# Attention on one NeuronCore: the exponential of a step taken head by head, each PSUM bank of the turned scores released by itself, layer-norm statistics one step later

## The chip, the cores and the metric

The kernel runs on one NeuronCore of a Trainium2 chip. The metric is the device time of one execution in microseconds (us). The engines are TensorE (PE; PEld is its weight load), VectorE (DVE), ScalarE (ACT), GpSimd (POOL) and SyncE (SP, which here only issues DMAs). They run side by side and wait for each other by semaphores.

## The reference

Two blocks, each of a cross attention and a feed-forward part, with layer norm ahead of each and a gain by tanh. The change lies in the first attention:

```python
# x, ctx_2048: (64, 64, 256) fp32; x is (batch, channel, position)
x = x + tanh(g_xattn[0]) * _L0_xattn_ref(_layernorm(x, axis=-1), ctx_2048, Wq, bq, Wk, bk, Wv, bv, Wo, bo)

def _L0_xattn_ref(x, c, ...):                 # 8 heads of 8 channels
    q, k, v = _proj(Wq, bq, x), _proj(Wk, bk, c), _proj(Wv, bv, c)
    q, k = _rope(q, 4), _rope(k, 4)           # per head, over 256 positions
    scores = einsum('bhqd,bhkd->bhqk', q, k) / sqrt(8)
    out = einsum('bhqk,bhkd->bhqd', softmax(scores), v)
    return _proj(Wo, bo, out)
```

Behind it follow a mixture of 8 experts (2 taken) with a shared one, a gated recurrent unit with pooled context, and a feed-forward part with a Hadamard rotation. The change leaves these alone.

## The kernel before, in words

**Tiles and steps.** Two batches make a tile of 128 rows (`TILES` = 32). A tile has 16 heads (8 of each batch), two to a step, so `STEPS` = 8 steps, called p = 0 to 7. Each engine walks through all tiles and steps with its own program (`body(n, c, i)`). Work on a tile is spread over several passes: in pass n, k and v come from tile n + 3 and n + 2, q from n + 2, plain scores from n + 1, turned scores from n or n − 1 (`LAG` = 5 steps behind), values two steps behind those, output of n − 2. Thirteen passes are written out (`PEEL_FIRST`, `PEEL_LAST`); 24 tiles run in a hardware loop of four passes a turn, where thresholds of semaphores are computed in registers.

**Scores twice.** A head's scores are computed in two layouts. *Plain*, with queries on partitions, into `s_ps` (two buffers of two PSUM banks): VectorE takes their row maximum (`take_max`, L400). *Turned*, with keys on partitions, into `st_ps` (one buffer, two banks, one a head): ScalarE takes the exponential into `e_t` (L461 to L468), with the maximum already taken off by rows of the stacked operand. TensorE then multiplies `e_t` by the values into `o_ps` (`use_values`, L557). The contraction of a score has 32 rows, so a head sits in one of four 32-row groups of TensorE's array; a step's two heads are in neighbouring groups, and the turned and plain heads of a step in different ones.

**TensorE's order in a step** (`score_step`, L531, then `use_values`, then one odd job on the bank `misc`). It waits until the exponential of the step before is done (all of `st_ps` is read) and until a buffer of `s_ps` is free, then issues eight matmuls: two turned (first half of the rows, both heads), two plain, two turned (second half), two plain. `st_scored` and `scored` go up once a step, with the last matmul of each kind. The odd jobs: p = 0 and 4 turn o (L577), p = 1 turns the maxima (L599), p = 2 projects q and p = 5 projects k (L508), p = 3 turns a (L617), p = 6 projects the output (L638), p = 7 projects v (L647).

**VectorE in a step**: the row maximum of two heads (L406, 128x1024), and around it at p = 0 the splitting of the maxima (L395, L397) and o's scaling (L412, L416), at p = 2 the layer-norm statistics of tile n + 3 (`stats_of`, L354) and behind them the rotary product of q (L387), at p = 4 o's scaling, at p = 5 the rotary product of k.

**ScalarE in a step**: the exponential, and behind it at p = 1 the copy of the maxima (L473), at p = 2 and 6 the copy of o (L478), at p = 3 that of a (L482), at p = 6 the output (L486), at p = 7 the copy of v (L494). Every second exponential also waits for `pv_done`, so that its buffer of `e_t` is free.

**POOL** normalizes and splits q's and k's inputs (L275, L301); **SP** issues the DMAs that stack q and k in row groups, and waits for `st_scored` of a whole tile ahead of overwriting a stacked buffer (L228, L256).

Of the kernel before, what the change touches and what calls it, by code (L numbers as in the profile page):

```python
# [19 lines left out]
HEADS, DH = 8, 8  # L20
# [47 lines left out]
def attention(nc, dram, x, ident, tanh_gain):  # L68
# [17 lines left out]
    with ExitStack() as ctx:  # L86
# [107 lines left out]
        def _(sp):  # L194
# [20 lines left out]
            def body(n, c, i):  # L215
# [9 lines left out]
                if there(n, c, 2):  # L225
                    r = (c + 2) % RING

                    wait_count(sp, s["st_scored"], STEPS * (n - 1))  # L228
                    if isinstance(n, int) and n == -2:
                        sp.wait_ge(s["q_first_cleared"], 1)  # L230
                    elif isinstance(n, int) and n < 2:
                        sp.wait_ge(s["q_cleared"], n + 2)
                    wait_alone(sp)
                    sp.dma_start(q_st[r][MAX_ROWS, :, :].bitcast(F32), zero_rows[:, :, :].bitcast(F32))\
                        .then_inc(q_stacked[r], 16)
# [17 lines left out]
                if there(n, c, 3):  # L253
                    r = (c + 3) % RING

                    wait_count(sp, s["st_scored"], STEPS * n)  # L256
                    sp.wait_ge(s["k_high"], n + 4)
# [87 lines left out]
        def _(dve):  # L345
# [76 lines left out]
            def body(n, c, i):  # L422
                for p in range(STEPS):
# [4 lines left out]
                    if p == 0 and there(n, c, -2):  # L428
                        normalize_out(n - 2, 1)
                    if p == 2 and there(n, c, 3):  # L430
                        stats_of(n, c, i, 3)
# [23 lines left out]
        def _(act):  # L455
# [3 lines left out]
            def body(n, c, i):  # L459
                for p in range(STEPS):  # L460
                    k, t = later(p, LAG)  # L461
                    if there(n, c, k):
                        g = STEPS * (n + k) + t
                        act.wait_ge(s["st_scored"], g + 1)
                        if t % 2 == 0:
                            wait_count(act, s["pv_done"], 2 * UNITS * (n + k) + 2 * (t // 2) - 2)
                        nc.scalar.activation(e_t[t % 4][:], st_ps[:], ACT.Exp, scale=float(DH) ** -0.5)\  # L467
                            .then_inc(s["exp_done"], 1)  # L468
                    if p == 1 and there(n, c, 0):
# [31 lines left out]
        def _(pe):  # L501
# [10 lines left out]
            def scores(c, p):  # L512

                r = (c + 1) % RING
                for half_ in range(2):
                    for at in range(2):
                        u, j = (2 * p + at) // UH, (2 * p + at) % UH
                        rows = slice(32 * j, 32 * j + 32)
                        yield (s_ps[p % 2][:, at, half_, :], q_st[r][rows, u, half_ * P:(half_ + 1) * P],
                               k_st[r][rows, u, :])  # L520

            def scores_turned(c, k, t):

                r = (c + k) % RING
                for half_ in range(2):
                    for at in range(2):
                        u, j = (2 * t + at) // UH, (2 * t + at) % UH
# [3 lines left out]
            def score_step(n, c, i, p):  # L531
# [3 lines left out]
                if turned:  # L535
                    if t == 0:
                        pe.wait_ge(m_stacked[(c + k) % RING], 16 * uses(c, i, k))
                    wait_count(pe, s["exp_done"], STEPS * (n + k) + t)
                    wait_alone(pe)
                if plain:  # L540
# [8 lines left out]
                    wait_count(pe, s["max_taken"], (n + 1) * STEPS + p - 1)  # L549
                for at in range(0, 4, 2):  # L550
                    for of, done in ((turned, "st_scored"), (plain, "scored")):
                        for out, w, moving in of[at:at + 2]:
                            last = nc.tensor.matmul(out, w, moving, start=True, stop=True)  # L553
                        if of and at == 2:
                            last.then_inc(s[done], 1)

            def use_values(n, c, p):  # L557

                k, t = later(p, LAG + 2)
                if there(n, c, k):  # L560
                    r, u, half_ = (c + k) % RING, t // 2, t % 2
                    if half_ == 0:
                        pe.wait_ge(s["exp_done"], STEPS * (n + k) + 2 * u + 2)
                        if u == 0:
# [1741 lines left out]
```

## Time and profile before

| | |
|---|---|
| median of 3 runs | 1506.12 us (1505.72 to 1512.41) |
| the profiled execution, in all | 1498.02 us |
| its span, from first to last instruction | 1496.0 us |
| PE, DVE, ACT, POOL busy over the span | 89%, 62%, 50%, 46% |
| exponentials (L467) | 256 of 1026 ns |
| row maxima (L406) | 256 of 1222 ns |
| mean granted TensorE clock | 0.964 |

Busy shares are means over four stages with different limits, and matmuls are pipelined, so that PE's share is no measure of its room. Attention is the stage up to about 513 us; what a change there is worth is read from its steps. The profile puts a step's records in order of time: start, length, engine, line, operation, what it writes and reads, and in brackets idle time ahead of it with what ended it.

### The profile page before, as it was taken

The page shows a single profiled execution, that of the slowest core. Times are in us where ns is not written, and L with a number is a line of the kernel's source. Part 1 is how long each engine was busy: PE and PEld are TensorE (multiplying, and loading weights), DVE is VectorE, ACT ScalarE, POOL GpSimd, SP SyncE. Part 2 cuts the span into 40 slices and gives each one's busy share as a digit, 9 for nine tenths or more (in the row PEclk, how much of TensorE's full clock was granted, in tenths as well). Part 3 has the DMA queues.
Part 4 walks back from the last instruction along what each step waited for, and adds up shares of the span by engine and source line. Part 5 has one row for each costly group of instructions (what it writes and reads, how often), then busy time and mean ns, then how long its engine had stood idle before and what let it go on. Part 6 is the DMA issues. An engine that isn't in the chain of part 4 may idle for free. (4 is left out here: it accounts for less than half of the span.)

```text
span 1496.0 us, 31398 instructions
## 1 busy us (share of the span) xinstructions
PE 1335.2 (89%) x10082; PEld 1003.1 (67%) x10083; DVE 925.2 (62%) x1685; ACT 753.8 (50%) x1205; POOL 683.2 (46%) x850
## 2 busy tenths in 40 slices
PE   4898999999998759999898999999957799999998
PEld 3444444444454348887787888888855688888887
DVE  7788888888898268665654333333324566666653
ACT  0477776777777643332343333333324666666652
POOL 7576767676764027544465433200044444554220
PEclk9999999999999969999999999999965899999999
DMA  3222222222221022111654333211161011111000
GB/s 99 81 72 79 71 79 71 78 77 76 79 74 48 3 90 99 47 53 68 193 178 159 95 95 91 69 51 53 46 216 29 7 36 43 43 28 43 15 15 29
DMA packets 88480, 107.61 MB, mean 72 GB/s; under 512 B 11280, under 2 KB 79248, under 8 KB 87760
## 3 DMA queue, kind: packets, MB, share of 16 engines
q1 hardware_dynamic: 78656, 74.57, 15.8%
q0 software_dynamic: 9744, 31.99, 6.7%
q8 instruction: 47, 0.77, 0.2%
q14 instruction: 33, 0.27, 0.1%
HBM read 54.10 MB, written 25.03 MB: 53 GB/s over the span
## 5 line engine op out<-in xcount | busy, mean ns | idle before, releaser
L406 DVE TENSOR_REDUCE row_max<-s_ps 128x4 f32<-128x1024 f32 x256 | 312.2, 1222 | 49.5 <-PE s_ps L553 44.5
L467 ACT ACTIVATE e_t<-st_ps 128x1024 f32<-128x1024 f32 x256 | 262.7, 1026 | 140.3 <-PE st_ps L553 140.3
L553 PE MATMUL st_ps<-q_st,k_st 32*128 32x256 f32 x1024 | 130.8, 331 | 45.6 <-DVE row_max L406 18.6
L569 PE MATMUL o_ps<-e_t,v_st 128*32 128x256 f32 x2048 | 166.2, 397 | 0.0
L553 PEld LDWEIGHTS st_ps<-q_st,k_st 32*128 32x128 f32 x1024 | 80.3, 187 | 103.9 <-issue 65.0
L1731 POOL DMA_INDIRECT gathered_tail<-sorted_results,result_at x64 | 70.3, 1098 | 154.1 <-POOLq L2222 135.8
L553 PE MATMUL s_ps<-k_st,q_st 32*128 32x256 f32 x1024 | 130.7, 342 | 5.9 <-DVE row_max L406 3.6
L1968 DVE TENSOR_TENSOR h_all_tail<-silu_tail,u_ps_tail 128x512 f32<-128x512 f32 x64 | 43.9, 685 | 122.0 <-ACT silu_tail L1839 66.7
L1589 PE MATMUL y_ps_moe<-w_all_moe,xt_hi_moe 128*128 x568 | 112.2, 281 | 4.7 <-DVE xt_lo_moe L1407 4.7
L1413 DVE TENSOR_TENSOR h_all_moe<-silu_moe,u_ps_moe 128x512 f32<-128x512 f32 x71 | 48.8, 687 | 108.9 <-PE u_ps_moe L1567 108.9
L1091 ACT COPY y_sb_moe<-y_ps_moe 128x256 f32<-128x256 f32 x71 | 26.5, 373 | 163.0 <-PE y_ps_moe L1589 163.0
L1567 PE MATMUL g_ps_moe<-w_all_moe,xt_hi_moe 128*128 x284 | 106.8, 417 | 0.0
L1567 PE MATMUL u_ps_moe<-w_all_moe,xt_hi_moe 128*128 x284 | 101.2, 397 | 0.0
L1589 PEld LDWEIGHTS y_ps_moe<-w_all_moe,xt_hi_moe 128*128 128x128 f32 x568 | 91.8, 188 | 8.4 <-issue 5.6
L929 POOL DMA_INDIRECT sorted_rows<-xn_moe,slots_moe x64 | 64.0, 1000 | 57.3 <-DVE slots_moe L1202 40.0
L1403 DVE TENSOR_TENSOR xt_lo_moe<-t_ps_moe,xt_hi_moe 128x256 fp32r<-128x256 f32 x71 | 30.1, 424 | 92.3 <-ACT xt_hi_moe L1078 92.3
L553 PEld LDWEIGHTS s_ps<-k_st,q_st 32*128 32x128 f32 x1024 | 77.7, 193 | 7.8 <-DVE row_max L406 4.9
L1839 ACT ACTIVATE silu_tail<-g_ps_tail 128x512 f32<-128x512 f32 x64 | 38.0, 594 | 84.0 <-PE g_ps_tail L2127 83.8
L1589 PE MATMUL y_ps_moe<-w_all_moe,xt_lo_moe 128*128 x284 | 79.5, 280 | 0.0
L304 POOL TENSOR_TENSOR q_bare<-q_roped 128x256 f32<-128x256 f32 x32 | 23.2, 726 | 112.2 <-DVE q_roped L387 112.2
L2139 PE MATMUL y_ps_tail<-w_hi_tail,h_hi_tail 128*128 128x256 f32 x256 | 74.0, 289 | 0.5 <-DVE h_lo_tail L1975 0.5
L1749 POOL TENSOR_SCALAR a_tail<-a_tail 128x1024 f32<-128x1024 f32 x8 | 22.6, 2826 | 111.5 <-ACT a_tail L1818 111.5
(337 smaller groups left out, 3716.1 us busy)
## 6 DMA issues: line engine op xcount, KB each, us to landing
k_st<-k_part SPq DMA_DIRECT2D x96, 128.0 KB
q_st<-q_part SPq DMA_DIRECT2D x96, 128.0 KB
stage_moe<-in_experts POOLq DMA_DIRECT2D x21, 512.0 KB
rows_in_moe<-sorted_rows SPq DMA_DIRECT2D x71, 128.0 KB
sorted_results<-y_sb_moe SPq DMA_DIRECT2D x71, 128.0 KB
c_in<-in_ctx SPq DMA_DIRECT2D x32, 128.0 KB
x_sb<-in_x SPq DMA_DIRECT2D x32, 128.0 KB
xn_moe<-in_ctx SPq DMA_DIRECT2D x8, 512.0 KB
```

The lines of the kernel that those rows point to most:

```text
L406: nc.vector.tensor_reduce(out, s_ps[p % 2][:], AX_X, ALU.max).then_inc(s["max_taken"], 1)
L467: nc.scalar.activation(e_t[t % 4][:], st_ps[:], ACT.Exp, scale=float(DH) ** -0.5)\
L553: last = nc.tensor.matmul(out, w, moving, start=True, stop=True)
L569: last = nc.tensor.matmul(o_ps[32 * j:32 * j + 32, u % 2, :], v_st[r][:, half_, u * UH + j, :], e_t[(2 * u + j // 2) % 4][:, j % 2, half_, :],
L929: pool.indirect_dma_start(out=xs[:, :], out_offset=bass.IndirectOffsetOnAxis(ap=slots[:, w, GT * j + t:GT * j + t + 1], axis=0), in_=xn[j ...
L1413: nc.vector.tensor_tensor(h_all[c % 2][:], silu[c % 2][:], u_ps[c % 2][:], ALU.mult)\
L1567: last = nc.tensor.matmul(bank[c % 2][:], t[b][:, kc * P:(kc + 1) * P], w_flat[:, bass.ds(where + ((w * 3 + kc) * PIECE + base), FF)], sta ...
L1589: last = nc.tensor.matmul(y_ps[:, 2 * ((c - 1) % 2), :], h[:, m * P:(m + 1) * P], w_flat[:, bass.ds(where + ((w * 3 + 2) * PIECE + m * D), ...
L1731: pool.indirect_dma_start(out=gathered[r][:], out_offset=None, in_=ys[:, :], in_offset=bass.IndirectOffsetOnAxis(ap=result_at[:, q // GT, ...
L1839: nc.scalar.activation(silu[m % 2][:], g_ps[n % 2][:], ACT.Silu).then_inc(s["silu_done"], 1)
L1968: nc.vector.tensor_tensor(h_all[m % 2][:], silu[m % 2][:], u_ps[n % 2][:], ALU.mult)\
L2139: last = nc.tensor.matmul(y_ps[:, t, :], h[:, m, t * P:(t + 1) * P], w[:, m * D:(m + 1) * D], start=(m == 0 and b == 0 and t % 2 == 0), st ...
```

## The change

The exponential of a step becomes two, one for each head, that is, for each bank of `st_ps`; each waits for its own count of `st_scored`, and raises `exp_done`. TensorE issues the score matmuls head by head: both halves of head 0, turned and plain in turn, then both of head 1. Ahead of the first it waits for the first exponential of the step before, ahead of head 1 for the second. All thresholds of the two semaphores double. VectorE's layer-norm statistics move from p = 2 (ahead of q's rotary product) to p = 3 (behind the row maximum of that step).

```diff
@@ SyncE: body
-                    wait_count(sp, s["st_scored"], STEPS * (n - 1))
+                    wait_count(sp, s["st_scored"], 2 * STEPS * (n - 1))
...
-                    wait_count(sp, s["st_scored"], STEPS * n)
+                    wait_count(sp, s["st_scored"], 2 * STEPS * n)
@@ VectorE: body
-                    if p == 2 and there(n, c, 3):
+                    if p == 3 and there(n, c, 3):
                         stats_of(n, c, i, 3)
@@ ScalarE: body
-                        act.wait_ge(s["st_scored"], g + 1)
                         if t % 2 == 0:
                             wait_count(act, s["pv_done"], 2 * UNITS * (n + k) + 2 * (t // 2) - 2)
-                        nc.scalar.activation(e_t[t % 4][:], st_ps[:], ACT.Exp, scale=float(DH) ** -0.5)\
-                            .then_inc(s["exp_done"], 1)
+                        for b in range(2):
+                            act.wait_ge(s["st_scored"], 2 * g + b + 1)
+                            nc.scalar.activation(e_t[t % 4][:, b, :, :], st_ps[:, b, :, :], ACT.Exp, scale=float(DH) ** -0.5)\
+                                .then_inc(s["exp_done"], 1)
@@ TensorE: scores, and the same in scores_turned
-                for half_ in range(2):
-                    for at in range(2):
+                for at in range(2):
+                    for half_ in range(2):
@@ TensorE: score_step
-                    wait_count(pe, s["exp_done"], STEPS * (n + k) + t)
+                    wait_count(pe, s["exp_done"], 2 * (STEPS * (n + k) + t) - 1)
...
-                for at in range(0, 4, 2):
-                    for of, done in ((turned, "st_scored"), (plain, "scored")):
-                        for out, w, moving in of[at:at + 2]:
-                            last = nc.tensor.matmul(out, w, moving, start=True, stop=True)
-                        if of and at == 2:
-                            last.then_inc(s[done], 1)
+                for at in range(4):
+                    if turned:
+                        if at == 2:
+                            wait_count(pe, s["exp_done"], 2 * (STEPS * (n + k) + t))
+                        out, w, moving = turned[at]
+                        last = nc.tensor.matmul(out, w, moving, start=True, stop=True)
+                        if at % 2 == 1:
+                            last.then_inc(s["st_scored"], 1)
+                    if plain:
+                        out, w, moving = plain[at]
+                        last = nc.tensor.matmul(out, w, moving, start=True, stop=True)
+                        if at == 3:
+                            last.then_inc(s["scored"], 1)
@@ TensorE: use_values
-                        pe.wait_ge(s["exp_done"], STEPS * (n + k) + 2 * u + 2)
+                        pe.wait_ge(s["exp_done"], 2 * (STEPS * (n + k) + 2 * u + 2))
```

## Rows read from the trace of the kernel before

**Rows 1.** The page's 40 slices of 37.4 us: tenths of the full clock
```profile
PEclk9999999999999969999999999999965899999999
```

**Rows 2.** Line L467 from 80 to 430 us: ns min/median/max; then idle us, times
```profile
L467 ACT ACTIVATE e_t<-st_ps x191: 1024/1025/1036, 79.6 to 429.5; 128x1024 f32<-128x1024 f32 x191
...
  PE st_ps L553: 96.6, 167
```

**Rows 3.** Timeline of PE, 252.3 to 258 us: start, length, engine, line, operation
```profile
252.36 0.39 PE L553 MATMUL st_ps<-q_st,k_st 32*128 32x256 f32 x2
252.37 0.38 PE L553 MATMUL s_ps<-k_st,q_st 32*128 32x256 f32 x2
252.58 0.28 PE L553 MATMUL st_ps<-q_st,k_st 32*128 32x256 f32 x2
...
252.80 0.64 PE L569 MATMUL o_ps<-e_t,v_st 128*32 128x256 f32 x8
253.37 0.66 PE L577 MATMUL misc<-ident,o_sb 128*128 128x128 f32 x4
254.17 0.38 PE L553 MATMUL st_ps<-q_st,k_st 32*128 32x256 f32 x2
...
255.18 0.39 PE L508 MATMUL misc<-k_input_high,w_high 128*128 128x256 f32 x1
...
255.87 0.28 PE L508 MATMUL misc<-k_input_low,w_high 128*128 128x256 f32 x1
256.08 0.39 PE L553 MATMUL st_ps<-q_st,k_st 32*128 32x256 f32 x2
...
257.09 0.70 PE L638 MATMUL misc<-a_t,w_out 128*128 128x256 f32 x2
```

**Rows 4.** Timeline of ACT in the same tile
```profile
252.90 1.03 ACT L467 ACTIVATE e_t<-st_ps 128x1024 f32<-128x1024 f32 x1 [0.26 <-PE st_ps L553]
254.78 1.02 ACT L467 ACTIVATE e_t<-st_ps 128x1024 f32<-128x1024 f32 x1 [0.85 <-PE st_ps L553]
...
258.01 0.58 ACT L486 ACTIVATE y_sb<-misc,out_bias,tanh_gain 128x256 f32<-128x256 f32 x1
258.47 1.03 ACT L467 ACTIVATE e_t<-st_ps 128x1024 f32<-128x1024 f32 x1
```

**Rows 5.** Timeline of all engines: the odd jobs of steps 3 and 7
```profile
251.79 0.44 PE L617 MATMUL misc<-ident,a_sb 128*128 128x128 f32 x2 [0.15 <-DVE q_roped L387]
...
258.89 0.71 PE L647 MATMUL misc<-w_in,c_in 128*128 128x128 f32 x4
```

**Rows 6.** Groups of instructions, 0 to 560 us and the page's part 5: 128x512 on ACT
```profile
L478 ACT COPY o_sb<-o_ps 128x512 f32<-128x512 f32 x64 | 37.1, 580 | 1.2 <-PE o_ps L569 1.2
...
L1839 ACT ACTIVATE silu_tail<-g_ps_tail 128x512 f32<-128x512 f32 x64 | 38.0, 594 | 84.0 <-PE g_ps_tail L2127 83.8
```

**Rows 7.** Timeline of DVE at steps 2 and 3; waits, 80 to 430 us
```profile
250.38 0.42 DVE L357 BATCH_NORM_STATS2 stats<-x_sb 128x6 f32 x1
...
251.04 0.69 DVE L387 TENSOR_TENSOR q_roped<-misc,rope 128x512 f32<-128x512 f32 x1
251.65 2.51 DVE L406 TENSOR_REDUCE row_max<-s_ps 128x4 f32<-128x1024 f32 x2
...
PEld misc L617 <- DVE q_roped L387: 14.8, 24, 0.6
```

**Rows 8.** Timeline of PE in tiles written out: the maxima; a step without odd job
```profile
438.97 0.30 PE L599 MATMUL misc<-ident,m_parts 128*64 128x128 f32 x1
...
487.40 0.38 PE L553 MATMUL st_ps<-q_st,k_st 32*128 32x256 f32 x2
...
489.10 0.38 PE L553 MATMUL st_ps<-q_st,k_st 32*128 32x256 f32 x2 [0.63 <-ACT e_t L467]
```

**Rows 9.** Timeline of PE ahead of 63 us
```profile
44.84 0.58 PE L553 MATMUL st_ps<-q_st,k_st 32*128 32x256 f32 x2
...
45.22 0.41 PE L553 MATMUL st_ps<-q_st,k_st 32*128 32x256 f32 x2
```

More of the change, by code:

```diff
@@ L524, in scores_turned @@
                 r = (c + k) % RING
-                for half_ in range(2):
-                    for at in range(2):
+                for at in range(2):
+                    for half_ in range(2):
                         u, j = (2 * t + at) // UH, (2 * t + at) % UH
```

## The prediction

> **What bounds the kernel now.** The change lies in attention alone, so I read that stage. The slices of the page put it in the first 34% of the span: to about 513 us, with a granted clock of nine tenths or more, which is the level of 2.4 GHz [rows 1]. How often does the work repeat? One line's view gives 191 exponentials from 79.6 to 429.5 us, so 349.9 / 190 = 1.842 us a step and 14.73 us a tile of eight steps [rows 2]. The same view says that ScalarE sat idle 96.6 us before 167 of them, always for the turned scores. It is not ScalarE's work that bounds, but a round trip through it. The timelines show the trip [rows 3, 4]: turned-score matmuls start at 252.36, the exponential starts at 252.90 (0.54 later), runs 1.03, ends at 253.93, and the next turned scores start at 254.17 (0.24 later). Sum 1.81, and the step is 1.81. All four `st_ps` matmuls wait for the whole exponential.
>
> TensorE bounds the other kind of step. In every step, by its start: four score matmuls in four row groups start together at 0, four more at 0.22, the values at 0.44, and the odd job (`misc`) at 1.01 [rows 3]. A projection's records run from 255.18 to 256.15, and the next step starts at 256.08, 0.07 before that end; no exponential held it (it ended at 255.80). That step takes 1.91. So TensorE's floor of a step is 1.01 + record of the odd job − 0.07. With 0.66 (o turned, twice), 0.30 (maxima), 0.97 (two projections), 0.44 (a turned), 0.70 (output), 0.71 (v) [rows 3, 5, 8]: 8 × 0.94 + 5.41 = 12.9 us a tile. Six steps at the round trip's 1.8, two at 1.91, and some more for queue waits at the tile's turn give the 14.73. The floor is 1.8 below it: that is what a shorter trip can win at most.
>
> **The change, part by part.**
>
> *Exponential by head.* 256 activations of 128x1024 become 512 of 128x512. The trace has none of that exact form. Nearest are the 128x512 silu of 594 ns and the copy of 580 ns [rows 6]; I take 0.60. Two of them back to back overlap: y_sb starts at 258.01, runs 0.58, and the exponential behind it starts at 258.47, 0.12 before its end [rows 4]. With 0.10 of overlap a pair lasts 1.10 against 1.025: +0.07 a step on ScalarE. Bounds: 1.06 (580 ns each) to 1.20 (no overlap). The Trainium skill, "ScalarE: Activation LUTs", section "What ACT_TABLE_LOAD costs", gives 186 ns + 0.833 ns per element with immediate scale and an overlap of about 93 ns: by it a pair is an estimated 1.13. The 1025 ns in this trace agrees with its formula; by 1.13 the gain below would be some 3 us smaller.
>
> *Each bank back by itself.* The first half's trip is now 0.54 + 0.60 + 0.24 = 1.38 instead of 1.81. The second half's matmuls of the next step wait for the second exponential. Counted from a step's start: 0.54 + 1.10 = 1.64, and 0.07 for a wait on the weight load itself (q_roped ends at 251.73, the matmul behind it starts at 251.79 [rows 5, 7]; up to 0.17 where the loop computes a threshold in a register ahead of it): 1.71. Behind this new wait on TensorE's queue lie the last four score matmuls, the values, the odd job and the next step. So what is late next is TensorE itself.
>
> *The matmuls' order.* Before, the four that start together have four different row groups. Now the stream is head 0 of both kinds, first half, then second half, then head 1: neighbours of one kind share a row group. Two matmuls can start, then four (second halves of head 0, first halves of head 1), then two: three beats instead of two. A beat is 0.11 (six projection matmuls start 0.69 apart from first to last, which with the first's own weight load is 0.12 each; 0.22 between the two starts of scores is a weight load and a matmul) [rows 3]. So TensorE pays +0.11 a step, 8 × 0.11 = 0.88 a tile. Bounds: nothing, if the row groups drift apart without loss, and +0.22, if the four pairs run one behind the other. I take 0.11, the value that the present beats give. The Trainium skill, "TensorE: Matmul & The Clock Gate", Part 3, says that a weight load overlaps running matmuls only when the row group differs. It speaks against this order; no row here has two neighbouring score matmuls in one row group, so the trace neither bears it out nor denies it.
>
> *Statistics one step later.* Before, VectorE does them ahead of q's rotation: 250.38, rotation at 251.04 [rows 7]. They hold q_roped some 0.4 us, and TensorE waited 14.8 us in 24 times (0.6 each) for it ahead of turning a. Now that wait goes; on the old trip it cost nothing, on a step bound by TensorE it would cost 0.2 to 0.4. The statistics then delay the next reductions. VectorE has room: 8 reductions of 1.14 net (1.23 less the 0.09 by which the next starts early), two rotations 1.2, statistics 0.57, output scaling 1.0, splitting of the maxima 0.4: 12.3 a tile. Pool gets the statistics 1.2 later, but needs them only behind four operations on q. I cost this move at nothing. If the cover is gone (the scaling of o at step 4 late, k's projection behind it) it is 0.1 a tile.
>
> *Semaphore counts doubled, register arithmetic, SyncE's waits.* The DMA waits mean the same events as before. Nothing, but for the 0 to 0.1 above.
>
> *Sum for a tile in the loop.* Step lengths are the larger of three: first trip 1.38; TensorE 1.05 + record (0.94 + 0.11); and, where the second half waits, 0.94 + record counted from its late start. In tile order (steps 0 to 7) TensorE gives 1.71, 1.35, 2.02, 1.49, 1.71, 2.02, 1.75, 1.76: 13.81. The late second half adds where a short step precedes: step 1 is only 1.38 long, so step 2's second half starts at 1.71 − 1.38 = 0.33 instead of 0.11 (+0.22); after step 3, 1.71 − 1.49 = 0.22 (+0.11). Step 6 holds ScalarE with the pair (1.64), o (0.48) and y (0.47), so step 7's first exponential is late and step 0's second half with it (+0.1). 13.81 + 0.03 + 0.43 = 14.27. That takes odd jobs other than projections to let go 0.07 before their records' end too, which no row shows; if each of those six lets go 0.05 later, 14.55. I take 14.4: 0.33 less than 14.73, × 24 tiles in the loop = 7.9 us.
>
> *Tiles written out.* There no register is computed between wait and matmul and a step is 1.70 [rows 8]; a loaded tile gains nothing. In the tail the projections are gone and some steps have no odd job. They follow the exponential alone (0.63 of waiting for it, [rows 8]): 1.70 falls to 1.3 to 1.5, some 2.5 us over the last three tiles. At the start two half-loaded tiles win about 1 us. In the first passes a beat lasts nearly twice as long (0.38 from the first to the second start at 45 us [rows 9], 0.22 later), though the page shows no lower clock there; some 5 steps bound by TensorE pay 0.2 more: a loss of 1 us. The stages behind attention start earlier and are otherwise as before.
>
> Sum: −7.9 − 2.5 − 1 + 1 = about −10 us. The profiled execution has a span of 1496.0 and 1498.02 in all: 1488. The median of the runs shown is 1506.12, 8 above it; the gain carries over in us: **1496**.
>
> **The rivals.**
> *A, the forecast.* Tile 14.27 to 14.57, −5 to −18 us: 1488 to 1501. For it: the trip is what ends last in six of eight steps.
> *B, the new wait costs more than a wait on a load.* 0.17 in place of 0.07, at every second half that waits: +0.25 a tile, so 14.65 and −3 us: 1503. For it: in the loop 0.24 lies between exponential and matmul, in the tiles written out 0.14 (a step of 1.70 against 1.80, [rows 3, 8]).
> *C, slower: four pairs one behind the other, and a pair of exponentials without overlap.* TensorE's block of scores and values grows by 0.22, the second trip to 0.54 + 1.20 + 0.17 = 1.91, and what follows the second half grows with it. The floor goes from 12.9 to 12.9 + 8 × 0.22 = 14.7, the late second halves and odd jobs that let go later (0.3) add 0.55: tile 15.25, +0.52 × 24 = +12.5, less 1.5 in the tail, plus 1 at the start: 1518 (1514 to 1524). It decides where a second half starts over 0.33 behind the first in most steps. Against it: every ScalarE pair in [rows 4] overlaps by 0.12.
> *D, the order costs nothing.* +0 for +0.11: tile 14.1, −20 us: 1486.
> *E, one row group's loads wait out its matmuls.* Each head's two halves are then 0.22 apart and no other head's come between: TensorE's block grows from 0.44 to 0.66, tile 14.8 to 15.1 with exponentials as in A: 1504 to 1513, likeliest 1508. For and against it: the floor of 12.9 alone becomes 14.7; but of the eight present matmuls four start at once.
> E is the rule of "TensorE: Matmul & The Clock Gate", Part 3, in the Trainium skill, taken in full.
>
> **How the numbers follow.** A 0.46, B 0.16, C 0.14, D 0.10, E 0.14. The likeliest gives 1496. Leaving out a tenth on either side: low 1485 (D's), high 1519 (inside C). About 0.5% (7.5 us) is what a measurement can tell here. Faster by more: D and 0.36 of A, 0.46. Within: the rest of A, B and 0.08 of E, 0.34. Slower by more: C and 0.06 of E, 0.20.
>
> **What would show it.** In the changed profile: 512 exponentials of about 0.60; a second one that starts 0.10 before the first's end; first turned scores 0.24 behind the first exponential, so no step but projections over 1.85. Three starts of score matmuls in a step, 0.11 apart, and values at 0.55 from the start; at 0.66 it is E or C. Turning a waits no longer for q_roped. Period of a tile 14.4 from one line's first and last start. The prediction is wrong if values start at 0.66 or later in a step that waited for no exponential, if a pair of exponentials takes 1.2, or if a wait on VectorE appears ahead of the scores.

## The result

The changed kernel took 1481.61 us (median of 4 runs, 1477.36 to 1486.68); the kernel before 1505.92 (4 runs). The ratio is 0.984, with a 95% interval of 0.9807 to 0.9873. The forecast of 1496 had the sign and was too small: 24.3 us were won instead of 10, and the time lies below the range (1485 to 1519).

| profiled execution | before | after |
|---|---|---|
| in all, us | 1498.02 | 1483.34 |
| span | 1496.0 | 1481.4 |
| attention over at (last exponential's end) | 514.8 | 488.7 |
| behind that | 981.2 | 992.7 |
| a tile in the loop | 14.73 | 14.04 |
| PE / DVE / ACT busy over the span | 89 / 62 / 50% | 91 / 62 / 52% |

Attention is 26 us shorter; 11.5 of them are missing in this one profile because the unchanged stages behind it took 992.7 us, the longest of all profiles here (below).

The page's costliest groups of the kernel after:

```profile
L468 ACT ACTIVATE e_t<-st_ps 128x512 f32<-128x512 f32 x512 | 278.5, 598 | 109.2 <-PE st_ps L556 103.5
L406 DVE TENSOR_REDUCE row_max<-s_ps 128x4 f32<-128x1024 f32 x256 | 311.9, 1220 | 30.0 <-PE s_ps L561 28.0
L556 PE MATMUL st_ps<-q_st,k_st 32*128 32x256 f32 x1024 | 158.2, 330 | 8.3 <-ACT e_t L468 3.6
```

The exponential's line in the kernel after, 80 to 430 us; to be set against [rows 2]:

```profile
L468 ACT ACTIVATE e_t<-st_ps x400: 591/597/627, 79.7 to 429.9; 128x512 f32<-128x512 f32 x134
...
  PE st_ps L556: 77.5, 110
```

400 halves in 350.2 us: 350.2 / 399 × 16 = 14.04 us a tile. ScalarE still waits for turned scores, but 110 times and not 167, and 77.5 us and not 96.6.

TensorE's timeline of the kernel after, end of step 2, step 3 and the start of step 4; to be set against [rows 3]:

```profile
208.26 0.28 PE L509 MATMUL misc<-q_input_low,w_high 128*128 128x256 f32 x1
...
208.47 0.38 PE L556 MATMUL st_ps<-q_st,k_st 32*128 32x256 f32 x1
208.47 0.38 PE L561 MATMUL s_ps<-k_st,q_st 32*128 32x256 f32 x1
208.49 0.38 PE L556 MATMUL st_ps<-q_st,k_st 32*128 32x256 f32 x1
208.49 0.38 PE L561 MATMUL s_ps<-k_st,q_st 32*128 32x256 f32 x1
208.69 0.27 PE L556 MATMUL st_ps<-q_st,k_st 32*128 32x256 f32 x1
208.70 0.27 PE L561 MATMUL s_ps<-k_st,q_st 32*128 32x256 f32 x1
208.71 0.28 PE L556 MATMUL st_ps<-q_st,k_st 32*128 32x256 f32 x1
208.71 0.28 PE L561 MATMUL s_ps<-k_st,q_st 32*128 32x256 f32 x1
208.92 0.64 PE L577 MATMUL o_ps<-e_t,v_st 128*32 128x256 f32 x8
209.49 0.44 PE L625 MATMUL misc<-ident,a_sb 128*128 128x128 f32 x2
209.85 0.38 PE L556 MATMUL st_ps<-q_st,k_st 32*128 32x256 f32 x1
...
210.08 0.28 PE L556 MATMUL st_ps<-q_st,k_st 32*128 32x256 f32 x1
...
210.14 0.38 PE L556 MATMUL st_ps<-q_st,k_st 32*128 32x256 f32 x1
...
210.37 0.27 PE L556 MATMUL st_ps<-q_st,k_st 32*128 32x256 f32 x1
...
210.57 0.64 PE L577 MATMUL o_ps<-e_t,v_st 128*32 128x256 f32 x8
```

Three things are to be seen. Step 3 is 1.38 long (208.47 to 209.85), where it was 1.80. Its eight score matmuls start four and four, 0.22 apart, and the values 0.45 behind the first (0.44 before): as before, without the third beat (a third start, 0.11 later) that the prediction charged. And in step 4 head 1's matmuls start 0.29 behind head 0's (210.14), because they wait for the second exponential, which ends at 210.08 (209.00 + 1.08, below); the values then come at 0.72.

ScalarE's timeline of the kernel after, steps 1 to 3 of one tile, and step 3 of the next, the one above; to be set against [rows 4] and [rows 6]:

```profile
191.44 1.09 ACT L468 ACTIVATE e_t<-st_ps 128x512 f32<-128x512 f32 x2 [0.62 <-PE st_ps L556]
192.41 0.25 ACT L474 CAST m_rows<-misc 64x128 fp32r<-64x128 f32 x1
192.81 1.09 ACT L468 ACTIVATE e_t<-st_ps 128x512 f32<-128x512 f32 x2
193.80 0.59 ACT L479 COPY o_sb<-o_ps 128x512 f32<-128x512 f32 x1
195.01 1.08 ACT L468 ACTIVATE e_t<-st_ps 128x512 f32<-128x512 f32 x2 [0.62 <-PE st_ps L556]
...
209.00 1.08 ACT L468 ACTIVATE e_t<-st_ps 128x512 f32<-128x512 f32 x2 [0.62 <-PE st_ps L556]
```

A pair takes 1.09 (two of 0.60, overlapping by 0.10); 1.10 was forecast.

### The profile page after: what moved, and what is told of

It is laid out like the page before. It is cut to its first block and busy times, and to the rows that moved or that the text cites. A ratio compares the mean times of both kernels' runs of the same rounds, so it can differ in the third digit from the quotient of the medians.

```text
span 1481.4 us, 31918 instructions
## 1 busy us (share of the span) xinstructions
PE 1353.9 (91%) x10082; PEld 1029.7 (70%) x10083; DVE 920.5 (62%) x1685; ACT 765.3 (52%) x1461; POOL 682.0 (46%) x850
## 5 line engine op out<-in xcount | busy, mean ns | idle before, releaser
L468 ACT ACTIVATE e_t<-st_ps 128x512 f32<-128x512 f32 x512 | 278.5, 598 | 109.2 <-PE st_ps L556 103.5
L556 PE MATMUL st_ps<-q_st,k_st 32*128 32x256 f32 x1024 | 158.2, 330 | 8.3 <-ACT e_t L468 3.6
L561 PE MATMUL s_ps<-k_st,q_st 32*128 32x256 f32 x1024 | 156.2, 339 | 5.1 <-DVE row_max L406 3.6
L556 PEld LDWEIGHTS st_ps<-q_st,k_st 32*128 32x128 f32 x1024 | 103.4, 184 | 60.0 <-issue 45.7
L561 PEld LDWEIGHTS s_ps<-k_st,q_st 32*128 32x128 f32 x1024 | 101.9, 191 | 7.1 <-DVE row_max L406 4.7
L1094 ACT ACTIVATE silu_moe<-g_ps_moe 128x512 f32<-128x512 f32 x71 | 42.4, 598 | 58.5 <-PE g_ps_moe L1575 58.5
```

Source lines behind the costliest of these rows:

```text
L468: nc.scalar.activation(e_t[t % 4][:, b, :, :], st_ps[:, b, :, :], ACT.Exp, scale=float(DH) ** -0.5)\
```

## The experiments

Each tile length below is worked out as above from the exponential's line, 80 to 430 us. The kernels were run in three sets, each with the kernel before on the same chip; ratios are to that one. The ratios are the record's and differ by up to 0.3 points from the quotient of the two medians.

### One part at a time

**order_only**, ratio 1.0045 (1.0022 to 1.0068). Loops of `scores` and `scores_turned` turned as in the change, and

```diff
-                for at in range(0, 4, 2):
+                for at in range(4):
                     for of, done in ((turned, "st_scored"), (plain, "scored")):
-                        for out, w, moving in of[at:at + 2]:
+                        for out, w, moving in of[at:at + 1]:
                             last = nc.tensor.matmul(out, w, moving, start=True, stop=True)
-                        if of and at == 2:
+                        if of and at == 3:
                             last.then_inc(s[done], 1)
```

> The kernel before with one part of the change: the score matmuls go head by head, turned and plain in turn. One exponential a step, one release, statistics where they were. Theory of the prediction (a third beat of 0.11 a step): the exponential starts 0.65 behind the first score matmul instead of 0.54, the tile is 8 x 0.11 = 0.88 longer, 15.6 us, and the whole 24 to 28 us longer: 1530 to 1534. Theory formed on the trace of the changed kernel (matmuls of one row group are held back and those of other groups drawn ahead, so that four start at once as before): exponential at 0.54, tile 14.73, 1506 (within 3). A third, that an order with two neighbours in one row group costs a whole weight load (0.22): 1555.

Measured: +0.45%, tile 14.87 (+0.13). TensorE's timeline of order_only, one step:

```profile
241.27 0.38 PE L553 MATMUL st_ps<-q_st,k_st 32*128 32x256 f32 x1
...
241.29 0.38 PE L553 MATMUL st_ps<-q_st,k_st 32*128 32x256 f32 x1
241.29 0.38 PE L553 MATMUL s_ps<-k_st,q_st 32*128 32x256 f32 x1
241.50 0.28 PE L553 MATMUL st_ps<-q_st,k_st 32*128 32x256 f32 x1
...
241.72 0.64 PE L569 MATMUL o_ps<-e_t,v_st 128*32 128x256 f32 x8
```

Two starts of four within 0.02, at 0 and 0.22 to 0.24, though the third and fourth matmul of the stream have the row groups of the first and second. Where head 1 is kept back by its own wait, the two halves of head 0, which share a row group, start 0.23 apart (209.85 and 210.08 in step 4 above), though nothing else keeps the second. So the two that start with the first pair are those of head 1: they went ahead of held-back ones. The prediction's +0.88 a tile is refuted, and so is the whole-load theory. What is left is 0.13 a tile: the exponential starts some 0.02 later behind the first score matmul (0.56 instead of 0.54), as the last turned matmul starts at 0.24 instead of 0.23. Attention as a whole is over at 517.1 us, 2.3 later than before.

**order_blocks**, ratio 1.0039 (1.0010 to 1.0068). As order_only, but

```diff
+                for of, done in ((turned, "st_scored"), (plain, "scored")):
+                    for out, w, moving in of:
+                        last = nc.tensor.matmul(out, w, moving, start=True, stop=True)
+                    if of:
+                        last.then_inc(s[done], 1)
```

> The kernel before with the score matmuls head by head as in the change, but all four turned ones ahead of all four plain ones (row groups a a b b c c d d in place of a c a c b d b d), one exponential. Theory (TensorE draws work of free row groups ahead over held ones through the whole block): two starts of four as ever, exponential 0.54 to 0.57 behind the first matmul, tile 14.7 to 14.9, ratio 1.00 to 1.005. Rival (it starts matmuls in order and waits at a busy row group): five beats, exponential at 0.65, values at 0.77 instead of 0.44, tile 16.2 to 17, ratio 1.03 to 1.05.

Measured: tile 14.79 (+0.06). TensorE's timeline of order_blocks, one step:

```profile
199.95 0.39 PE L552 MATMUL st_ps<-q_st,k_st 32*128 32x256 f32 x2 [0.32 <-DVE row_max L406]
199.96 0.39 PE L552 MATMUL s_ps<-k_st,q_st 32*128 32x256 f32 x2
200.17 0.28 PE L552 MATMUL st_ps<-q_st,k_st 32*128 32x256 f32 x2
200.19 0.28 PE L552 MATMUL s_ps<-k_st,q_st 32*128 32x256 f32 x2
200.40 0.64 PE L568 MATMUL o_ps<-e_t,v_st 128*32 128x256 f32 x8
```

The plain matmuls are the fifth to eighth of the stream here, and two of them start 0.01 behind the first. So the reach is the whole block of eight, and two starts of four come out of any of the three orders. The total rose by 0.39%, some 6 us, of which 24 × 0.06 = 1.4 us lie in the loop's tiles; the rest is not traced to the order.

**split_only**, ratio 1.0112 (1.0058 to 1.0166).

```diff
-                        nc.scalar.activation(e_t[t % 4][:], st_ps[:], ACT.Exp, scale=float(DH) ** -0.5)\
-                            .then_inc(s["exp_done"], 1)
+                        for b in range(2):
+                            last = nc.scalar.activation(e_t[t % 4][:, b, :, :], st_ps[:, b, :, :], ACT.Exp, scale=float(DH) ** -0.5)
+                        last.then_inc(s["exp_done"], 1)
```

> The kernel before with the exponential as two activations of 128x512, both behind one wait, released together after the second. It gives the price of the split alone. Theory (pair of 1.09 to 1.10 instead of 1.025, on the trip that ends six of eight steps): +0.07 x 6 = +0.42 a tile in the loop, as much in the tiles written out: +13 us, 1519. Rival (no overlap between two exponentials, pair 1.20): +0.17 x 6 = +1.0 a tile, +32: 1538. Rival (the odd jobs hide it): 1506.

Measured: 1511.64 against 1498.25, +13; the exponential's line of split_only, 80 to 430 us:

```profile
L468 ACT ACTIVATE e_t<-st_ps x370: 590/598/629, 80.4 to 429.0; 128x512 f32<-128x512 f32 x185
```

348.6 / 369 × 16 = 15.12: +0.39 a tile, 9.4 us in the loop's 24 tiles. The theory holds: the price of splitting is what a pair is longer, on the trip.

**stats_only**, ratio 1.0001 (0.9973 to 1.0029): `p == 2` to `p == 3` for `stats_of`, nothing else.

> The kernel before with the statistics one step later and nothing else. Theory (step 3 is set by the trip through ScalarE, the wait of turning a for q_roped has slack): no change, 1506 (within 3); the wait of L617 for q_roped is gone from the list of waits. Rival (the 5.9 us that the changed kernel has won by the start of the third tile's turned scores come from this part): 1500, first exponential of tile 2 at 72 us instead of 77.8.

Measured: tile 14.73, no change. L617's entry for q_roped did not vanish from the list of waits, as the expectation had it: it fell from 14.8 to 9.9 us in 24 times, 0.41 each, which is the idle that every odd job has ahead of it. The rival on the first tiles falls: the first exponential of tile 2 starts at 75.8 us, and in the kernels with the old trip at 75.8 to 77.8.

**release_together**, ratio 1.0094 (1.0071 to 1.0117). The whole change except the early release.

```diff
-                    wait_count(pe, s["exp_done"], 2 * (STEPS * (n + k) + t) - 1)
+                    wait_count(pe, s["exp_done"], 2 * (STEPS * (n + k) + t))
...
-                        if at == 2:
-                            wait_count(pe, s["exp_done"], 2 * (STEPS * (n + k) + t))
```

> The changed kernel, but the first score matmuls of a step wait for both exponentials of the step before; the second wait falls away. All else stays: two exponentials, each started by its own bank, order head by head, statistics at step 3. Theory (all the gain is the early release of the first bank): trip 0.54 + 1.09 + 0.24 = 1.87, as the split alone plus the order alone: tile 15.2, ratio to the kernel before 1.011 to 1.018. Rival (part of the gain comes from the exponentials' own early start or from the order): tile 14.3 to 14.8, ratio 0.99 to 1.00.

The exponential's line of release_together, 80 to 430 us:

```profile
L468 ACT ACTIVATE e_t<-st_ps x373: 591/597/627, 79.6 to 429.6; 128x512 f32<-128x512 f32 x187
```

350.0 / 372 × 16 = 15.05. Without the early release the change costs 15 us (1497.65 against 1482.55); with it, it gains 24 on the same chip. So the early release alone is worth 1.0 us a tile (15.05 to 14.05) and pays for everything else. The ratio came out 0.16 points under the low end expected, because split and order together cost 0.32 a tile and not 0.39 + 0.13. A likely reason, not tested by itself, is that the first exponential starts as soon as its own bank is scored. Of the 15 us, 24 × 0.32 = 7.7 lie in the loop. In the profile another part comes from the clock: behind 20 us in which TensorE was busy for 15.5 it was granted at 0.50 from 510 us on, the level of 1.2 GHz, and the last tile took 17.45 us instead of 13.12 in the kernel before. The windows view of release_together (stretch, length, PE busy, granted clock, DMA share, GB/s):

```profile
510.00:515.00 5.00, 4.69 (x32) 0.50 0.01 3
```

### The whole change again, and the place of the statistics

**changed_second** (the changed kernel), ratio 0.9843 (0.9820 to 0.9866).

> The changed kernel as it is, on the chip of the three others of this set and against the kernel before there. Attention itself ended 26.2 us earlier in its profile (488.6 against 514.8 us), the whole only 14.7, while the medians differ by 24. Theory (the stages behind attention run unchanged code, but their length changes by up to 10 us a run with the stretches at which the clock is granted at half; of this kernel's profile the rest was long): ratio 0.982 to 0.985, tile 14.03 again, attention ended at 488 to 492, and the rest different from the 992.8 us of the first profile, nearer to 980. Rival (an earlier end of attention lets the stages behind collide with something, 11 us are given back for good): the rest is 990 to 995 again.

Measured: 1458.94 against 1482.55, −23.6; tile 14.05; attention over at 490.7; the span 1456.9, so 966.2 behind it. In the first profile it was 992.7. The rival (11 us given back for good) is refuted. Over the profiles of all kernels here, whose code behind attention is the same, that rest is 965 to 993 us: 965 to 969 in the four of this set, 974 to 984 and 978 to 983 in the two others. So all four on this set's chip lie below all others. Within this set and the first of them the rest is longer where the mean granted clock of the execution is lower (965.0 at 0.964 to 969.2 at 0.955; 973.7 at 0.965 to 984.3 at 0.957), as the theory has it; the third set shows no such order. The last exponentials of the kernel before and after, and of this run, whole span (the last start plus its length is the end of attention):

```profile
L467 ACT ACTIVATE e_t<-st_ps x256: 1024/1025/1036, 43.4 to 513.8; 128x1024 f32<-128x1024 f32 x128
```

```profile
L468 ACT ACTIVATE e_t<-st_ps x512: 591/597/633, 42.7 to 488.1; 128x512 f32<-128x512 f32 x171
```

```profile
L468 ACT ACTIVATE e_t<-st_ps x512: 589/597/629, 42.8 to 490.1; 128x512 f32<-128x512 f32 x171
```

**no_stats**, ratio 0.9854 (0.9816 to 0.9893), 1474.90 against 1498.25, and **no_stats_second**, 0.9835 (0.9812 to 0.9858): the changed kernel with `stats_of` back at `p == 2`.

> The changed kernel with the statistics back at step 2, ahead of q's rotary product. Theory (the step is now set by TensorE, and turning a comes 0.4 later as it waits for q_roped): up to +0.4 a tile, step 3 of 1.75 instead of 1.38; 24 tiles in the loop and five others: +5 to +11, 1487 to 1493. Rival (what step 3 loses, the wait for the second exponential behind it gives back, so that nothing remains): 1481 (within 3).

> The changed kernel with the statistics left at step 2, beside the changed kernel on one chip. In its first profile the tile was 13.96 us, in that of the changed kernel 14.03. Theory (at step 3 the statistics hold up the next row maximum, o's scaling and with it k's projection; that costs more than the wait for q_roped at step 2 does): 0.07 x 28 = 2 us faster than the changed kernel, ratio of the two 0.9987, tile 13.96 again. Rival (both places cost the same): equal within 1 us. The prediction's statement that the move costs nothing would hold for the total, its reason (VectorE has room) would not for the step.

Measured: tile 13.95 and 13.97, 0.08 to 0.09 shorter than the changed kernel's; in the whole, in the second, 1459.53 against 1458.94, no difference. The theory of the first (+5 to +11) is refuted, with its reason: turning a does wait for q_roped (step 3 is 1.59 long instead of 1.38), but step 4's second half is then hardly late (its values come at 0.53 instead of 0.72), so the wait for the second exponential gives it back. Step 5 is 0.08 shorter besides, and that is the difference of the tiles. In the second, the tile is shorter as expected and the 2 us were not found in the total.

**stats_ahead**, ratio 0.9836 (0.9815 to 0.9857).

```diff
-                    if p == 3 and there(n, c, 3):
+                    if p == 3 and isinstance(n, int) and n == -3:
                         stats_of(n, c, i, 3)
+                    if p == 6 and there(n, c, 4):
+                        stats_of(n, c, i, 4)
```

> The changed kernel with the statistics taken out of steps 2 and 3 altogether: they are done at step 6, behind the row maximum, one tile earlier (tile n + 4 in pass n), where VectorE stood idle 0.3 to 0.5 us before the row maximum of step 7. Theory (either place costs: step 3 is held by q_roped 0.21 us with the statistics at step 2, k's projection at step 5 by o's scaling 0.07 to 0.16 us with them at step 3; here neither): tile 13.85 to 13.9, 3 to 5 us faster than the changed kernel. Rival (what is saved there is waited for at the second exponential of the next step): tile 13.95, 1 to 2 us.

Measured: tile 13.95, 1457.86 us, 1 us under the changed kernel: the rival. k's projection at step 5 no longer starts late (1.02 instead of 1.10 behind the step's start, on average), that is all. Of the 2 us that 24 shorter tiles give, none is left at the end of attention (490.9 against 490.7): its first exponential starts at 46.5 us instead of 42.8.

### What binds now

**half_second**, ratio 0.9713 (0.9675 to 0.9750).

```diff
@@ POOL: ahead of all (and a wait for e_cleared on TensorE)
+            for r in range(4):
+                nc.gpsimd.memset(e_t[r][:, 1, 1, :], 1.0).then_inc(s["e_cleared"], 1)
@@ ScalarE: body
-                            nc.scalar.activation(e_t[t % 4][:, b, :, :], st_ps[:, b, :, :], ACT.Exp, scale=float(DH) ** -0.5)\
-                                .then_inc(s["exp_done"], 1)
+                            h = 2 - b
+                            nc.scalar.activation(e_t[t % 4][:, b, 0:h, :], st_ps[:, b, 0:h, :], ACT.Exp,
+                                                 scale=float(DH) ** -0.5).then_inc(s["exp_done"], 1)
```

> The changed kernel with the second exponential of a step cut to half its elements: keys 128 to 255 of head 1 are left out of the exponential (that quarter of the buffer holds ones), so attention's result is another. All waits, matmuls and the first exponential stay. It shortens only what the second half of the next step's scores waits for. Theory (second halves of the scores start late at steps 2, 4, 7 and 0, by 0.28, 0.28, 0.06 and 0.18, as they wait for the second exponential; all other time is TensorE's): exponential 0.38 instead of 0.60, so late by 0.07 at steps 2 and 4 and nowhere else, tile 14.04 - 0.65 = 13.4, ratio to the kernel before 0.972. Rival (the late start is hidden or is VectorE's, and the tile is TensorE's sum already): tile 14.0, ratio 0.984.

ScalarE's timeline and the exponential's line, 80 to 430 us, of half_second:

```profile
248.08 0.87 ACT L471 ACTIVATE e_t<-st_ps 128x512 f32<-128x512 f32 x2 [0.79 <-PE st_ps L560]
```

```profile
L471 ACT ACTIVATE e_t<-st_ps x414: 376/505/617, 80.2 to 429.9; 128x512 f32<-128x512 f32 x69, 128x256 f32<-128x256 f32 x69
```

The pair is 0.87 long instead of 1.09, and the tile 349.7 / 413 × 16 = 13.55, 0.5 shorter (0.65 expected; k's projection now waits for o's scaling, and step 5 is 2.20 long on average instead of 2.00). The median is 1457.58 against 1498.48. So the second exponential, most of it through the second wait, is what the tile still pays beside TensorE's own work. Step 7 gains 0.13 of the 0.5, and there ScalarE's queue, which the shorter exponential also relieves, has a part.

**y_on_vector**, ratio 0.9802 (0.9770 to 0.9833), and **y_on_vector_s2**, 0.9787 (0.9752 to 0.9821), the latter with the statistics at step 2.

```diff
@@ ScalarE: body (wait for bias_ready added on VectorE)
-                    if p == 6 and there(n, c, -2):
-                        act.wait_ge(s["y_projected"], n - 1)
-                        act.wait_ge(s["y_free"], n - 1)
-                        nc.scalar.activation(y_sb[:], misc[:, 0:D], ACT.Identity, bias=out_bias[:],
-                                             scale=tanh_gain[:, 0:1]).then_inc(s["y_taken"], 1)
@@ VectorE: body
+                    if p == 6 and there(n, c, -2):
+                        dve.wait_ge(s["y_projected"], n - 1)
+                        dve.wait_ge(s["y_free"], n - 1)
+                        nc.vector.tensor_scalar(y_sb[:], misc[:, 0:D], tanh_gain[:, 0:1], out_bias[:], ALU.mult, ALU.add)\
+                            .then_inc(s["y_taken"], 1)
```

> The changed kernel with the output's scaling (128x256, 581 ns on ScalarE at step 6) moved to VectorE, behind the row maximum of step 6. Theory (ScalarE's second copy at step 6 starts step 7's exponentials 0.25 late, and with them the second halves at steps 0 and 7): late starts of 0.06 and 0.18 fall away, some 0.1 of queue at v's projection too: tile 13.8 to 13.85, 5 us faster than the changed kernel, ratio to the kernel before 0.980. Rival (VectorE's row maximum of step 7 then comes 0.3 later and with it the scores of two steps on): tile 14.0 to 14.1, ratio 0.984 to 0.986.

> The same with the statistics left at step 2. Theory: as y_on_vector less the 0.07 a tile by which statistics at step 2 were the shorter in two profiles: tile 13.75, ratio 0.979. Rival (the place of the statistics moves nothing that can be measured in the whole): equal to y_on_vector within 1 us.

The exponential's line of y_on_vector, 80 to 430 us:

```profile
L474 ACT ACTIVATE e_t<-st_ps x406: 589/597/602, 79.7 to 429.9; 128x512 f32<-128x512 f32 x136
```

350.2 / 405 × 16 = 13.84, and 13.73 for the second, both as their theories say. Steps 0 and 7 are shorter by 0.13 and 0.07 on average, where the theory put the late starts. 1469.60 and 1470.54 against 1498.48: 28 to 29 us under the kernel before, where the changed kernel is 24 under. The intervals overlap with the changed kernel's (0.9843), so of the total the gain over the changed kernel is likely and not shown; the tile, 0.2 to 0.3 shorter, shows it. Between the two, the medians are 0.9 us apart: the second's rival, that the place of the statistics moves nothing in the whole, holds.

## Why the prediction was wrong, point by point

The words are the prediction's: the trip is the time from the turned scores through their exponential to the next turned scores, a beat the time between two starts of score matmuls, the floor what TensorE's own work takes in a tile.

- **What bounds, and the trip: right.** 0.54 to the exponential, 0.24 behind it, and 1.38 for the first half: step 1 is 1.37 long. (Step 3 is 1.38 long, but there TensorE's own work, 0.94 + 0.44, gives the same.) release_together shows that the early release is what shortens the tile. The sign "no step but projections over 1.85" did not come true: step 4 is 1.88 long, by the second wait.
- **Exponential by head: right.** 0.60 each, 1.09 a pair; split alone +13 us.
- **The matmuls' order, +0.11 a step: the step that failed.** It is 0.88 of a tile's sum. The prediction charged three starts of score matmuls in a step; order_only and order_blocks show two in any order, and 0.13 and 0.06 a tile in place of 0.88. I had taken neighbours in one row group for a reason to wait. But the stream as a whole offers four free row groups, and TensorE takes the free ones first, past the new wait too when that is met. What misled me is that in the kernel before program order and row groups happened to agree [rows 3], so that no row could tell "in order" from "by row group". That was said, and then 0.11 was taken as if the beats gave it. Rival D, no cost of order (14.1, 1486), had 0.10 of chance and was the true one. Against rival E (the loads of a row group wait out its matmuls) the trace of the kernel before did speak, though the prediction says that it neither bears the rule out nor denies it. TensorE's weight loads there:

```profile
252.35 0.19 PEld L553 LDWEIGHTS st_ps<-q_st,k_st 32*128 32x128 f32 x2 [0.36 <-issue]
...
252.46 0.19 PEld L553 LDWEIGHTS st_ps<-q_st,k_st 32*128 32x128 f32 x2
```

The second halves' loads start at 252.46, while the matmuls of the same row groups (252.36, 0.39 long) run.

- **TensorE's floor, and odd jobs letting go 0.07 before their record's end: right.** Step 3 runs 209.49 + 0.44 − 0.07 = 209.86, and the next starts at 209.85. The mean over the loop is 0.07 for every odd job behind which no wait ends last. The extra 0.05 for each of the other six, of which the forecast took a part (14.4 instead of 14.27), was not there. (Six times 0.05 on 14.27 is 14.57, as rival A has it, and not 14.55.)
- **Late second halves: right in kind, too small.** Forecast 0.43; in the trace some 0.28 (step 2), 0.28 (step 4), 0.06 (7) and 0.18 (0): 0.80. It is larger because without a third beat head 1 could start at 0.02 instead of 0.11, and step 3 is 1.38 instead of 1.49 long, while the second exponential ends at the same time after a step's start. The prediction's own terms with beats at nothing give 12.93 + 0.14 (step 1) + 0.33 + 0.33 + 0.1 = 13.83. Floor 12.93, + 0.80, + 0.15 (step 1 held by the first trip), + 0.1 (queue at steps 5 and 7): 13.98, measured 14.04.
- **Statistics: right that the total doesn't move**, in both surroundings. The reason, that VectorE has room, was not right for the step: there is a delay at either place. The 0.2 at step 3 is absorbed by the wait for the second exponential; the 0.08 at step 5 stays, near the 0.1 a tile that the prediction named for the case that the cover is gone. So by the tile the statistics were better left where they were; 24 × 0.08 = 2 us are too few to be seen in the total.
- **Written-out tiles: forecast 0, measured 0.25 each (3 tiles)**; without the third beat their steps shorten too. **Tail: 2.9, forecast 2.5.**
- **First passes: forecast 0 (1 won, 1 lost), measured 5.9 in the first profile**, up to the first exponential of tile 2 (71.9 us instead of 77.8). The kernel after, in its early passes:

```profile
44.19 0.58 PE L556 MATMUL st_ps<-q_st,k_st 32*128 32x256 f32 x1
...
44.58 0.41 PE L556 MATMUL st_ps<-q_st,k_st 32*128 32x256 f32 x1
...
50.63 0.38 PE L556 MATMUL st_ps<-q_st,k_st 32*128 32x256 f32 x1
...
50.86 0.27 PE L556 MATMUL st_ps<-q_st,k_st 32*128 32x256 f32 x1
```

The two starts of a head are 0.39 apart at 44 us and 0.23 at 50.6: TensorE's pace rose by a factor of 1.7 near 50 us, in the kernel before near 63. The views show a granted clock of 1.00 on both sides. But the trace's own record of the granted clock begins only at this point, at 50.4 us in the kernel after and 63.1 in the kernel before, with a grant of 1.0, the level of 2.4 GHz; that the stretch ahead of it ran at the level of 1.2 is inferred from the pace and not recorded. With the new trip the pace rose at 50, 55, 57, 59, 54, 53, 51 and 64 us in eight profiles, with the old one at 57 to 63 in six. Kernels with a rise at 57 to 59 us had reached tile 2 at 74.9 to 75.3 with the new trip and 75.8 to 76.6 with the old. So about 1 us (0.6 to 1.7) of the 5.9 is the trip; the rest goes with when the pace rose. Whether the denser start brings it forward or whether this was chance, these profiles leave open.

The sum of the first profiles: 24 tiles × 0.69 = 16.6, + 0.8 + 2.9 + 5.9 = 26.2 us in attention. The prediction's place in the profile was right and two terms of its sum wrong. With beats at nothing its own working comes to 1486 (rival D), and nearly all of what is still missing to 26 is the first passes, most of which may be chance. How much of the 24.3 us between the medians they make can't be told from one profile; in the second set the gain was 23.6, with the rise at 55 us in its profile.

## What to carry to other kernels

Where one engine's round trip through another ends last, releasing the buffer in halves pays even if the halves cost more in sum: here +0.39 and +0.13 a tile for a gain of 1.0. After it, cost every step against two bounds, the engine's own sum and the second half's release; a step shortened to the first half's trip makes the next one's second half late. And a cost taken from the order in which work starts needs a row in which the order differs from the other explanation; where none is, neither end of its bounds is given by the rows, and the chances should say so.

## What the runs showed of the hardware that was not expected

In these traces TensorE does not start matmuls in program order when they lie in different row groups. In order_blocks two plain matmuls, which come fifth and later in the block, start 0.01 us behind the first, and two turned ones, which come ahead of them, 0.22 behind it. By the row groups the two plain ones are the fifth and seventh, and the second of the block, which shares the first's row group, is held back. The Trainium skill, "TensorE: Matmul & The Clock Gate", Part 3, says that weight loads of a row group that isn't in conflict are pulled ahead (by that rule, the trace agrees: where no wait keeps head 1 back, all of a block's loads start within 0.13 us), and also that matmuls start strictly in program order; the starts above speak against the second. It says too that a load overlaps running matmuls only when the row group differs; here the second load of a row group starts 0.11 us behind the first (208.58 and 208.47), while that group's first matmul (208.47, 0.38 long on record) runs. A load that carries a wait for a semaphore is pulled ahead as well once the wait is met: in the changed kernel head 1's matmuls, behind the new wait, start 0.02 behind head 0's first (208.49 and 208.47 in the timeline of the kernel after). The trace's semaphores tell them apart: the load that waits for `exp_done` starts at 208.48, and neither of the two matmuls that raise `st_scored`, one of which stands ahead of that load in the program, starts before 208.69. The loads of the turned scores in that step, kernel after:

```profile
208.47 0.18 PEld L556 LDWEIGHTS st_ps<-q_st,k_st 32*128 32x128 f32 x1
...
208.48 0.18 PEld L556 LDWEIGHTS st_ps<-q_st,k_st 32*128 32x128 f32 x1
...
208.58 0.18 PEld L556 LDWEIGHTS st_ps<-q_st,k_st 32*128 32x128 f32 x1
```

The rest of this kernel, unchanged code, took 965 to 993 us over the chips and executions of these runs. A gain of 1.6% is better read from the stage that was changed (26 us, or 0.69 a tile, with tiles of 14.04 and 14.05 in two profiles of the changed kernel) than from one profile's total (14.7).
